# Deformable convolutions on one core: distances made later in ACT's order, second unit's offsets in other PSUM banks, some loads behind

## What is computed

```python
def _block(x, dc_w, dc_b, of_w, of_b, dw, db):
    h = jax.nn.relu(_deconv2d(x, dc_w, dc_b))
    offset = _conv2d(h, of_w, of_b, PAD)
    return jax.nn.relu(_deform_conv2d(h, offset, dw, db))
...
for i in range(1, 4):
    in_cur = x + in_prev
    x = _block(in_cur, deconv_w[i], deconv_b[i], off_w[i], off_b[i], dcn_w[i], dcn_b[i])
    in_prev = in_cur
x_cat = jnp.concatenate((x, in_module), axis=1)
offset = _conv2d(x_cat, fin_off_w, fin_off_b, PAD)
return _deform_conv2d(x_cat, offset, fin_dcn_w, fin_dcn_b)
```

## Time and profile before

| | |
|---|---|
| median of three runs | 4506.23 us (4501.54 to 4509.08) |
| the profiled execution | 4504.67 us, its span 4502.9 us |
| granted PE clock, mean | 0.918 |
| busy: PE, DVE, ACT, POOL | 88%, 65%, 62%, 25% |
| chain that ended last | PE 76%, SP's queue 9%, issue 6%, DMA 3%, ACT 3% |
| product, distance, copy: mean of one | 549 ns, 1252 ns, 444 ns |
| a load of 2 MB (`A<-x_dram`) | 10.3 us to landing |

### The profile page before, as it was taken

The page is one execution under the profiler, slowest core; times in us unless marked ns, Lnnn a source line. Parts: engine busy times, 40 slices in busy tenths (PEclk is TensorE's granted clock), DMA queues, the critical chain, the costliest instruction groups (busy, mean ns, idle before and its releaser), DMA issues.

```text
span 4502.9 us, 221715 instructions
## 1 busy us (share of the span) xinstructions
PE 3951.5 (88%) x81888; PEld 3022.6 (67%) x81888; DVE 2921.2 (65%) x5838; ACT 2777.9 (62%) x6651; POOL 1143.3 (25%) x655
## 2 busy tenths in 40 slices
PE   5998798799699879979969988986999998799998
PEld 3676576577477657657747765764777776677776
DVE  4785686588478568658847856863666663566665
ACT  2785587488388558748838856872555552455554
POOL 0341243144034124214403413420111110111110
PEclk8999899799899989979979998997999999899999
DMA  3442443344244244334424424436555553655554
GB/s 115 120 125 69 126 125 92 93 125 125 72 121 125 65 122 125 92 102 125 123 69 122 125 67 127 125 104 175 135 138 131 137 133 105 164 134 138 129 138 100
DMA packets 243253, 527.19 MB, mean 117 GB/s; under 512 B 61152, under 2 KB 151776, under 8 KB 225632
## 3 DMA queue, kind: packets, MB, share of 16 engines
q1 hardware_dynamic: 242880, 522.27, 44.6%
HBM read 465.57 MB, written 56.45 MB: 116 GB/s over the span
## 4 chain that ended last, share of the span: by engine, by line
PE 76%; SPq 9%; issue 6%; DMA 3%; ACT 3%; DVE 2%; POOLq 1%; POOL 0%; ACTq 0%; PEld 0%; PEldq 0%; DVEq 0%
PE P L539 30%; PE PS L557 28%; PE PS L570 9%; PE P L510 7%; SPq L395 4%; SPq L387 3%; DMA HB<-off_store 1%; ACT H L816 1%; PE PS L510 1%; ACT YC L752 1%; DVE FOFF L1000 1%; DMA off_store<-FOFF 1%; SPq L377 1%; DVE ST L1004 1%; DVE ST L1003 0%
## 5 line engine op out<-in xcount | busy, mean ns | idle before, releaser
L883 DVE TENSOR_TENSOR A<-P,YC 121x384 f32<-121x384 f32 (+1 forms) x4608 | 2310.6, 549 | 995.2 <-ACT YC L752 847.8
L539 PE MATMUL P<-HL,SEL 32*121 32x384 f16 (+1 forms) x21504 | 1752.2, 306 | 326.0 <-issue 161.5
L752 ACT ACTIVATE YC<-P 121x384 f32<-121x384 f32 (+1 forms) x4608 | 1732.0, 444 | 23.3 <-PE P L539 17.0
L539 PEld LDWEIGHTS P<-HL,SEL 32*121 32x121 f16 (+1 forms) x21504 | 1136.4, 117 | 718.1 <-issue 372.3
L557 PE MATMUL PS<-A,VT 121*32 121x80 f32 (+1 forms) x40960 | 1390.6, 252 | 31.9 <-ACT SMP L729 15.3
L557 PEld LDWEIGHTS PS<-A,VT 121*32 121x32 f32 (+1 forms) x40960 | 1134.3, 118 | 335.9 <-issue 192.7
L1064 POOL CAST HL<-DIST 128x1152 f16<-128x1152 f32 x320 | 365.6, 1143 | 3101.3 <-DVE DIST L888 3008.8
L729 ACT ACTIVATE SMP<-PS 128x480 f32<-128x480 f32 (+3 forms) x1152 | 592.7, 514 | 749.8 <-PE PS L557 744.6
L1066 POOL TENSOR_TENSOR HL<-DIST,HL 128x1152 f16<-128x1152 f32 x320 | 769.3, 2404 | 134.7 <-issue 75.5
L719 ACT ACTIVATE DIST<-HB,CONST 128x1152 f32<-128x1152 f32 x320 | 400.7, 1252 | 424.6 <-DMA HB<-off_store 214.3
L570 PE MATMUL PS<-SMP,CW 128*64 128x128 f32 x7424 | 475.9, 277 | 5.4 <-ACT SMP L729 5.4
(11 more groups left out here) (56 smaller groups left out, 584.0 us busy)
## 6 DMA issues: line engine op xcount, KB each, us to landing
HB<-off_store SPq DMA_DIRECT2D x2560, 72.0 KB
VT<-ht_store SPq DMA_DIRECT2D x256, 512.0 KB
VT<-ht_store SPq DMA_DIRECT2D x768, 132.0 KB
VT<-ht_store SPq DMA_DIRECT2D x256, 88.0 KB
off_store<-FOFF SPq DMA_DIRECT2D x160, 128.0 KB, 2.5
ht_store<-A SPq DMA_DIRECT2D x32, 256.0 KB, 3.3
ht_store<-VT SPq DMA_DIRECT2D x32, 256.0 KB, 3.2
A<-x_dram SPq DMA_DIRECT2D x2, 2048.0 KB, 10.3
```

The lines of the kernel that those rows point to most:

```text
L539: mm = nc.tensor.matmul(dst, SEL[q, table, 0:sh.npos], hats, start=part == 0, stop=part == 1)
L752: nc.scalar.activation(YC[0:sh.npos, g % X_SLOTS, 0:sh.size], P[0:sh.npos, g % Y_SLOTS, 0:sh.size], ACT.Copy).then_inc(y_ready, 1)
L883: return nc.vector.tensor_tensor(dst, x, y, ALU.mult)
```

## The change

- ACT makes the distance of chunk c+1 behind the copy of group `next_after` (1 in hidden steps, 4 in the first batch of final ones) instead of ahead of group 0, but ahead of the read that follows that group; DVE clamps it behind product `next_after` + 1.
- Hidden steps: unit 1's offsets go into banks 0 to 3, directly behind unit 0's; PE's transposes of unit 1 come last, into banks 4 to 7, after DVE has read unit 0.
- Final steps: PE transposes both sources first; unit 0's offsets go into banks 0 to 3, unit 1's into 4 to 7, with no wait for DVE. SP stores the transposed banks ahead of unit 0's offsets.
- SP: the loads of `X`, of the next group's normal input and of the next layer's convolution weights move from ahead of the barrier to behind the first windows and the offsets of chunks 2 and 3.

```diff
+        self.next_after = self.sum_after if self.batches == 1 else self.after[0]
...
                 load_windows(sh, 1, corners(0, 1))
                 next_offsets(2, 1, 0)
                 next_offsets(3, 1, 1)
+                later_loads()
                 with sp.Fori(0, BANDS - 2) as pair:
...
-                    for half in range(UNITS) if final and unit == 1 else [] if final else [unit]:
+                    for half in range(UNITS) if final and unit == 0 else [] if final else [unit]:
...
-                if final:
-
-                    sp.dma_start(X[:, bass.ds(group * XSIZE, PIX)],
-                                 t["x"][bass.ds(group * IMG, IMG)].rearrange("b c h w -> (b c) (h w)")).then_inc(x_back, 16)
                 for slot in range(OFF_SLOTS):
                     sp.wait_ge(off_stored[slot], 32 * ITEMS // OFF_SLOTS)
                 wait_alone(sp, ht_stored, 16 * BANKFULS * UNITS)
-                if final and group < GROUPS - 1:
-                    load_normal(group + 1)
-                if not final and group == GROUPS - 1:
-                    load_conv(layer + 1)
-                sampling(sp, bar_count, final, body_of, fallback)
+                def later_loads():
+
+                    if final:
+                        sp.dma_start(X[:, bass.ds(group * XSIZE, PIX)],
+                                     t["x"][bass.ds(group * IMG, IMG)].rearrange("b c h w -> (b c) (h w)")).then_inc(x_back, 16)
+                    if final and group < GROUPS - 1:
+                        load_normal(group + 1)
+                    if not final and group == GROUPS - 1:
+                        load_conv(layer + 1)
...
+                if final:
+
+                    for half in range(UNITS):
+                        transposes(4, 0, half, x_rows_all, free=0 if half else 4)
+                    wait_alone(pe, final_ready, group + 1)
+                    for half in range(UNITS):
+                        transposes(4, 1, half, H)
+                    for unit in range(UNITS):
                         if unit == 1:
+
+                            wait_alone(pe, ht_copied, 2 * UNITS * BANKFULS)
+                        conv_tiles(4 * unit, unit, W[:, 0, :], x_rows, True, False)
+                        conv_tiles(4 * unit, unit, W[:, 1, :], h_rows, False, True).then_inc(off_full, 1)
+                else:
+
+                    pe.wait_ge(conv_act, 8)
+                    pe.wait_ge(conv_dve, 8)
+                    transposes(0, 0, 0, H, free=4)
+
+                    wait_alone(pe, conv_act, 16)
+                    wait_alone(pe, conv_dve, 16)
+                    conv_tiles(4, 0, W[:, 1, :], h_rows, True, True).then_inc(off_full, 1)
+
+                    wait_alone(pe, ht_copied, BANKFULS)
+                    conv_tiles(0, 1, W[:, 1, :], h_rows, True, True).then_inc(off_full, 1)
+
+                    wait_alone(pe, off_ready, IMG)
+                    transposes(4, 0, 1, H, free=4)
...
-                            if b == 0 and g == 0 and not last:
-                                next_distance(c + 1, band + half, 1 - half)
                             act.wait_ge(y_full, n + 1)
...
+                            if b == 0 and g == sh.next_after and not last:
+                                next_distance(c + 1, band + half, 1 - half)
...
-                            if b == 0 and g == 1 and not last:
+                            if b == 0 and g == sh.next_after + 1 and not last:
                                 clamp(c + 1)
...
-                    nc.vector.scalar_tensor_tensor(FOFF[:, n % OFF_SLOTS, :], bank((0 if final else 4) + image), SCALE, PXB[:, :],
+                    nc.vector.scalar_tensor_tensor(FOFF[:, n % OFF_SLOTS, :], bank(4 * (unit if final else 1 - unit) + image), SCALE, PXB[:, :],
```

More of the change, by code:

```diff
@@ L430, in body_of, with fallback @@
                 next_windows(CHUNKS - 1, BANDS - 1, 1)
-            def fallback(sh):
+            def fallback(sh, later_loads):
                 T = turns(sh)
+                later_loads()
                 with sp.Fori(0, BANDS) as band:
@@ L481, in step @@
                 wait_alone(sp, ht_stored, 16 * BANKFULS * UNITS)
-                if final and group < GROUPS - 1:
-                    load_normal(group + 1)
-                if not final and group == GROUPS - 1:
-                    load_conv(layer + 1)
-                sampling(sp, bar_count, final, body_of, fallback)
+                def later_loads():
[6 more added lines that the diff above has]
+                        load_conv(layer + 1)
+                sampling(sp, bar_count, final, lambda sh: body_of(sh, later_loads), lambda sh: fallback(sh, later_loads))
                 if final:
@@ L513, in conv_tiles, with transposes @@
                 return mm
-            def transposes(bank0, s, unit, source):
+            def transposes(bank0, s, unit, source, free=0):
                 for n in range(BANKFULS):
                     use = (UNITS * s + unit) * BANKFULS + n
-                    if use >= 4:
+                    if n >= free:
                         pe.wait_ge(ht_copied, use - 3)
@@ L674, in step @@
                         conv_tiles(IMG * unit, unit, W[:, 0, :], x_rows, True, True).then_inc(conv_full, 1)
-                for unit in range(UNITS):
-                    if final:
-                        if unit == 1:
-                            wait_alone(pe, final_ready, group + 1)
-                        for half in range(UNITS):
-                            transposes(4, unit, half, H if unit else x_rows_all)
-                    else:
-                        pe.wait_ge(conv_act, 8 * unit + 8)
-                        pe.wait_ge(conv_dve, 8 * unit + 8)
-                        transposes(0, 0, unit, H)
-                        wait_alone(pe, conv_act, 16)
-                        wait_alone(pe, conv_dve, 16)
-                    if unit == 1:
-                        wait_alone(pe, off_ready, IMG)
-                    for s in range(sources):
-                        view = x_rows if final and s == 0 else h_rows
-                        if final and s == 1 and unit == 0:
-                            wait_alone(pe, final_ready, group + 1)
-                        mm = conv_tiles(0 if final else 4, unit, W[:, s if final else 1, :], view, s == 0, s == sources - 1)
-                    mm.then_inc(off_full, 1)
@@ L798, in keep_transposes @@
                         sources = 2 if final else 1
+                        slot = (4 if final else 4 * unit) + use % 4
                         act.wait_ge(ht_full, use + 1)
                         dst = staged(sources, unit, n, count).rearrange("p (l i s c) -> p s (l i) c", l=LANES, i=IMG, s=sources)
-                        nc.scalar.activation(dst[:, s], bank((4 if final else 0) + use % 4)[0:count, :].rearrange(
+                        nc.scalar.activation(dst[:, s], bank(slot)[0:count, :].rearrange(
                             "p (l c) -> p l c", c=CH), ACT.Copy).then_inc(ht_copied, 1)
```

2 lines of the change are left out of this document (1 added, 1 removed).

## The result

The changed kernel takes 4451.6 us (median of 4 runs, 4450.8 to 4455.4), the kernel before 4507.0 us in the same comparison. The ratio is 0.9873, 95% interval 0.9861 to 0.9884: 55 us faster, where 149 were forecast. The profiled span went from 4502.9 to 4448.9 us.

What follows compares the result with a forecast made beforehand. ACT's order of work (gap, then low clock) bounds final steps; SP's issuing bounds hidden steps by their end. Gains 115 + 22 + 4 (windows further ahead of PE) + 2 + 6 = 149 us: 4357 us, range 4320 to 4430.

Steps and rivals of the forecast that it cites:

- the loop in the hidden steps: Hidden steps, from hats through spreads, copies, distance and clamp to the next hats: 8.6 us a chunk, said to cost nothing.
- SP's 8.7 us: Hidden steps: SP's time per chunk to issue offset and window loads, taken as the bound by a step's end.
- The clamp moves back by a product as well: Hidden steps: DVE's later clamp delays POOL's hats, done 4.66 us after it; counted within the 8.6 us loop, no cost.
- hats bound the hidden loop: Rival, hidden steps: loop of 8.8 to 8.9 us or SP's start unmoved; 4385 us, or up to 4420; chance 0.09.
- the rival that ended slower: Rival, hidden steps: the hats' loop at 9.2 us or more eats the final steps' gain; some 4524 us at 9.3; chance 0.03.
- Final steps: 58 rounds lose the gap before sampling and the low clock behind it, 19.90 to 17.92 us each: 115 us gained.
- The floor of 17.79 us: Final steps: the last chunk's measured round, which makes no distance, taken as the least a round could take.
- The allowance of 0.13 us for the branch: Final steps: added to each round's 17.79 us for the loop's branch, which the last chunk lacks; could be 0 to 0.3.
- The rival in which the clock keeps falling: Rival, final steps: short waits still lower PE's clock, each round keeps about 1.5 us; gain 62 us, 4444; chance 0.12.
- Start of the hidden steps: ACT's earlier copies let SP issue chunk 2's windows sooner: 2.8 us a step, 22 us over eight, bounds 0 to 5.7.
- Banks and transposes: Hidden steps: PE no longer waits for DVE to read unit 0's offsets; 0.3 us a step, 2 us in all.
- Fronts of the final steps: Loads moved behind the first windows: 6 us gained in the first final step, 0 in the second; by the skill, none.

Runs made afterwards that it cites:

- add-behind-10 kernel: The changed kernel, but in hidden steps DVE adds the residual behind product 10 instead of product 3: 4391.1 us.
- other edits only: The changed kernel with distance and clamp back in their old places in all steps, the rest of the change kept: 4497.5 us.
- banks' edit only: The kernel before plus only unit 1's offsets in other banks and its transposes behind; distances, clamps and loads in their old places: 4495.8 us.
- hidden distance as before: The changed kernel, but in hidden steps distance and clamp stand where the kernel before had them; final steps stay changed: 4371.8 us.
- the two versions with the distance behind copy 0: The changed kernel with the hidden steps' distance behind group 0's copy, clamp behind product 1: 4360.4 us; the same with the residual add behind product 10: 4361.3 us.
- the add behind 10 and the half low pass: The add-behind-10 kernel, with POOL's second pass (low part of the hats) over only the first half of the distances, in all steps: 4330.1 us.
- the joined loads: Distance behind copy 0 and add behind product 10, with each image's two offset loads joined into one, in final steps too: 5852.8 us.
- the two kernels above: The kernels other edits only (loads behind the first windows), 4497.5 us, and banks' edit only (loads ahead of the barrier), 4495.8 us.
- the run with half of the offset loads: Distance behind copy 0 and add behind product 10, with the x offsets not loaded from chunk 2 on in hidden steps: 4288.6 us.

## Why the prediction was wrong, step by step

**The step that failed** is the loop in the hidden steps: "8.6 us. That is just under SP's 8.7 us, so it costs nothing". Two things were wrong in it. The loop from hats to hats is 8.72 us (add-behind-10 kernel): 0.12 us longer than I summed; from hats to clamp it is 4.07 us, not 3.9. And it was laid beside the wrong pace. SP's 8.7 us was read rightly: in all eight hidden steps of the kernel before its windows come 8.68 to 8.71 us apart over chunks 10 to 28. But PE starts a step behind SP and catches up only because its own rounds are shorter, 8.57 us (8.56 in the prediction). In the first step it samples chunk 3 7.0 us behind the end of its windows' issue, chunk 15 4.3 us and chunk 29 2.3 us; in the other seven it is still 2.4 to 4.3 us behind at chunk 29. It waited for windows twice in all eight steps, 0.8 us. So the hats' loop had to stay under PE's own 8.57 us, not under SP's 8.7. At 8.7 us a round PE hardly catches up. SP and PE in the add-behind-10 kernel, the windows of chunk 29 and their sampling, beside the earlier trace rows:

```profile
367.69 19.03 SPq L397 DMA_DIRECT2D VT<-ht_store  x12
...
377.36 1.04 PE L563 MATMUL PS<-A,VT 121*32 121x80 f32 x48
```

SP took 3.99 us to issue these windows, up to 371.68, and PE comes 5.7 us behind that, where in the kernel before it came 2.3 us behind. The step ends later by it. It costs 266.6 - 262.6 = 4 us a step, 32 us in all.

The 262 to 263 us of a hidden step are thus of two kinds. In the kernel before, other edits only, banks' edit only and hidden distance as before, they are PE's own rounds of 8.57 us, which end about where SP does. In the two versions with the distance behind copy 0, and with the add behind 10 and the half low pass, PE is faster, catches up in mid-step and waits: 36.6, 56.6 and 94.3 us for windows. There the prediction's reading holds, that a faster PE gains nothing in the end.

**What was left out** is the larger part. "The clamp moves back by a product as well" followed the clamp to POOL, but not what then stands behind it on DVE. The residual add kept its place, one product nearer to the clamp, and took 0.47 us longer in each chunk, held up by POOL's pass. That costs 274.7 - 266.5 = 8 us a step, 65 us. It could be read in the trace of before: an add of 128x128 that took 0.61 us in hidden steps and 0.34 in the final ones. In the rival (hats bound the hidden loop, 4380 to 4420 us, chance 0.09) the direction was right and the mechanism half right; the measured loss, 95 us, is beyond its 35 and nearer to that of the rival that ended slower. (That rival's sum has a slip: 0.5 x 29 x 8 is 116, not 121; the 121 us of 115 + 6 are eaten at 9.22 us a round.)

**Final steps** were right in mechanism and a little small: rounds of 17.70 us on average, 17.92 forecast; 128 us for 115. Gap and low clock, the two parts that were named, are both gone. The floor of 17.79 us from the last chunk was no floor: every other round takes 17.51. The allowance of 0.13 us for the branch wasn't needed. The rival in which the clock keeps falling did not come: 1.00 over both steps, so the outcome that the Trainium skill (TensorE: Matmul & The Clock Gate, section "A second HAM failure mode: psum-queue depth-cycling") would have given does not show in this trace.

**Start of the hidden steps.** Forecast 2.8 us a step sooner. In the first step the windows of chunk 2 were issued at 131.88 instead of 135.12, 3.2 us, and the order on ACT is the one that was told:

```profile
123.00 0.49 ACT L761 ACTIVATE YC<-P 121x384 f32<-121x384 f32 x1 [0.19 <-PE P L545]
123.38 1.25 ACT L730 ACTIVATE DIST<-HB,CONST 128x1152 f32<-128x1152 f32 x1
...
126.89 0.57 ACT L740 ACTIVATE SMP<-PS 128x480 f32<-128x480 f32 x1 [1.12 <-PE PS L563]
```

The first read of samples comes at 126.89 for 129.56, forecast 126.6. But this agreement is luck. With the hidden distance as before, that read comes at 127.16 and the windows of chunk 2 go out at 131.39, sooner still; so nearly all of the 3.2 us comes from elsewhere. Counted from a step's first windows, those of chunk 2 follow after 24.7 us on average over the eight steps, 25.3 with the hidden distance as before and 25.4 in the kernel before: 0.6 us a step is what the distance gives there, not 2.8. Over the later steps the gap between two steps shrank by 1.6 us; with the first step 14.6 us in all, where 22 were forecast. The part in the gaps is the distance's, not the banks': with the hidden distance as before, or with the other edits only, the gap is 110.6 and 110.7 us, as in the kernel before. Why a step then gains more than 0.6 us was not taken apart. One step's rows had been taken for all eight.

**Banks and transposes.** 2 us forecast (bounds 0 and 7), some 10 measured alone (8 in the profiled execution). Too small. The gaps between hidden steps, where I had put it, are unchanged (110.9 us); in the profile 2.4 us lie ahead of the first sum, 3.3 between the final steps, 2.4 within the hidden steps. The first two are hardly more than such fronts differ between profiles (the first sum comes at 131.9 to 134.7 us in the kernels with the other edits and whole hats, the joined loads aside; for the fronts between final steps see above), so where the 10 us lie stays open, and so do the waits that gave them.

**Fronts of the final steps.** 6 us forecast, 5.6 measured, which agree as a total only. By the two kernels above the loads gave 4.6 us in the first final step (forecast 6) and cost 4.3 in the second (forecast 0), but the first stands barely clear of the spread between profiles (130.3 against 131.2) and the second inside it. In the second front the rows follow the working. SP's queue:

```profile
3843.13 6.67 SPq L397 DMA_DIRECT2D VT<-ht_store  x8
3849.84 8.63 SPq L389 DMA_DIRECT2D HB<-off_store  x16
3858.51 0.42 SPq L486 DMA_DIRECT2D X<-x_dram  x1
```

and DVE at chunk 1:

```profile
3876.77 2.42 DVE L895 TENSOR_TENSOR A<-P,YC 128x384 f32<-128x384 f32 x5 [11.19 <-DMA X<-x_dram]
```

From the last sum of the step before to the first windows: 3843.13 - 3770.56 = 72.6 us, before 3839.23 - 3758.0 = 81.2. These 8.6 us are what was forecast (8.7; 3.6 of them come with the banks' edit alone), and X takes most of it back: chunk 1's products start 33.6 us behind the windows instead of 26.8. What is won in front of the barrier is paid at the wait for X. In the kernel with the banks' edit only, loads ahead, the first windows of the second final step come 77.6 us behind the last sum, in all kernels with the loads behind, the joined loads aside, after 71.0 to 73.9 us. So their place does matter there for what stands in front of the barrier; the Trainium skill (DMA: Bandwidth & Descriptors, section Queues, rings and completion order), by which code for the restart would not stand behind X's load, doesn't explain these 4 us, and what the front waited for isn't shown. In the first final step the same distance is 82.6 and 84.6 us with the loads ahead and 82.2 to 87.3 with the loads behind: no difference shows. In their sum the moved loads gave nothing that can be measured, which is the total that the prediction had worked out from the Trainium skill for them.

**The sum again, with what was measured:** 128 + 15 + 6 - 95 = 54 us. With the hidden distance left in its old place the gain was 140 us, and 152 with it behind copy 0: the size that had been forecast, but by another kernel.

**The better version.** Final steps as changed, hidden steps with the distance behind copy 0: 4360 us, 3.3% under before and 91 us under the changed kernel. The next bound is SP's queue, 8 x (262.2 - 254.4) = 62 us by the run with half of the offset loads.

## What to carry to other kernels

When an instruction moves in one engine's order, look at its new neighbours as well as at its consumers: whatever stood behind it now meets the other engines at another moment. An instruction that takes twice as long in one part of the program as in another, with the same shape, tells of a resource that it waits for; find out whose, before anything near it is moved. Lay a new loop beside the rounds that an engine really makes, not beside those of a queue that it hasn't caught up with yet: who waits for whom, and from which chunk on, tells which it is. And where two loops lie within 0.1 to 0.2 us of each other, neither is "covered": price the move by both.

## What the runs showed of the hardware

- A DVE add of 128x128 with both inputs in SBUF, begun while POOL reads SBUF, ends 0.15 us behind POOL's instruction, whether that leaves it 0.61, 1.08 or 2.27 us; by itself it takes 0.34 us. DVE products with one input in PSUM don't: three take 1.49 us with a pass beside them or without.
- A DMA whose source has three dimensions (2 x 16 x 1152 elements, the middle one with step 0), joined from two of two dimensions, took 0.72 us of SP's queue in the median but up to 6.9, the four of a chunk 7.1 to 8.5 us. While they were under way the DMA engines were busy 0.12 to 0.13 and moved 51 to 53 GB/s. ACT waited 892 us for such loads, against 102 us in the changed kernel.
- With the gap of 1.3 us before the sampling gone, PE's granted clock stayed at 1.00 through 547 us of a final step, although PE's weight loads still waited some 480 times, 0.2 us on average. With the gap, 24 of 31 rounds had a stretch of 0.50, which made them 1.7 us longer than those without.
